# A gated recurrent step with sigmoid gates and one scan, and small work moved between engines, in a four-layer graph kernel

## The reference

```
layer 0:   per edge (i, j): g = exp(coeff*(e_ij - offsets)^2), h = ssp(W1 g + b1), Wf = W2 h + b2
           y_i = sum_j  A_ij^2 * Wf_ij * (Wa r_j);  out = Wd2 ssp(Wd1 y + bd1) + bd2
layer 1:   scores = QK/sqrt(128) + adj; softmax over the 8 largest; weighted sum of V; layer norm
layer 2:   graph attention with leaky scores, masked softmax, normalisation
layer 3:   d = row sum of (adj + I);  d_inv = d > 0 ? d^-0.5 : 0;  agg = d_inv * (adj + I) * d_inv @ x
           dyn = conv1d(x);  LSTM over the 128 positions of dyn, batch 64:
               z = W_ih x_t + b_ih + W_hh h + b_hh;  i, f, g, o = split(z)
               c = sigmoid(f)*c + sigmoid(i)*tanh(g);   h = sigmoid(o)*tanh(c)
           out = sigmoid(agg @ all h)
```

## Time and profile before

| | us |
|---|---|
| median of three runs (1372.89 to 1377.21) | 1374.94 |
| the profiled execution | 1368.68 |
| its span, from the first to the last instruction | 1366.4 |
| PE busy (share of the span) | 1142.1 (84%) |
| DVE busy | 927.6 (68%) |
| ACT busy | 908.8 (67%) |
| POOL busy | 686.5 (50%) |
| mean granted TensorE clock, share of full | 0.957 |

### The profile page before, as it was taken

How to read it: one execution, slowest core, us unless ns; L and a number is a source line. 1 busy time by engine, 2 the same in 40 slices (tenths; PEclk the granted TensorE clock), 3 DMA queues, 4 the chain that set the end, 5 groups by cost and what they waited for, 6 DMA issues and landing times. The chain is left out here.

```text
span 1366.4 us, 28761 instructions
## 1 busy us (share of the span) xinstructions
PE 1142.1 (84%) x5996; PEld 752.7 (55%) x6028; DVE 927.6 (68%) x3952; ACT 908.8 (67%) x2636; POOL 686.5 (50%) x1146
## 2 busy tenths in 40 slices
PE   2588889898988888988925789989789999999984
PEld 1244445555544554555514577777666666666673
DVE  3599998988898988889724888788423333333357
ACT  2488888778788878778812778878544444444467
POOL 5266665656665656656755899998500000000026
PEclk9999999999999999999965999999999999999988
DMA  1788677677777886767700111111000000000003
GB/s 47 162 182 193 167 191 168 174 186 163 172 188 167 187 171 173 191 160 177 172 6 21 34 38 39 32 40 32 16 1 0 0 0 0 0 0 0 0 23 102
DMA packets 128163, 129.04 MB, mean 94 GB/s; under 512 B 60867, under 2 KB 107359, under 8 KB 128097
## 3 DMA queue, kind: packets, MB, share of 16 engines
q1 hardware_dynamic: 126372, 127.19, 38.8%
q10 hardware_dynamic: 1725, 1.13, 0.3%
HBM read 123.05 MB, written 5.21 MB: 94 GB/s over the span
## 5 line engine op out<-in xcount | busy, mean ns | idle before, releaser
L782 PE MATMUL wf<-hid,w2t 128*128 128x384 f32 x512 | 209.3, 534 | 61.6 <-DVE msg L957 61.6
L569 POOL TENSOR_TENSOR sum<-msg 128x384 f32<-128x384 f32 (+1 forms) x128 | 146.5, 1145 | 74.4 <-DVE msg L957 73.9
L782 PEld LDWEIGHTS wf<-hid,w2t 128*128 128x128 f32 x512 | 89.9, 195 | 138.3 <-issue 106.5
L1787 POOL MEMSET r_minus_half<- 128x4 f32 x1 | 0.1, 102 | 324.7 <-POOLq L1653 324.7
L957 DVE SCALAR_TENSOR_TENSOR msg<-wf,b2c,rv 128x768 f32<-128x768 f32 x128 | 130.0, 1015 | 14.6 <-PE wf L782 14.2
L1735 DVE SCALAR_TENSOR_TENSOR r_new<-r_gates 128x64 f32<-128x64 f32 x128 | 28.9, 226 | 149.9 <-ACT r_gates L1715 149.9
L682 ACT ACTIVATE expd<-zb,safe_b,reached 128x768 f32<-128x768 f32 x128 | 124.9, 976 | 1.8 <-PE zb L768 1.8
L930 DVE TENSOR_TENSOR rv<-rg,sq_bc 128x768 f32<-128x768 f32 x128 | 121.4, 948 | 1.7 <-PE rg L811 1.4
L1681 PE MATMUL r_zgo<-xin,w_hh 128*128 (+1 forms) x508 | 110.2, 299 | 14.0 <-DVE xin L1744 1.8
L687 ACT ACTIVATE hid<-expd 128x768 f32<-128x768 f32 x128 | 108.0, 844 | 17.7
L767 PE MATMUL zb<-gauss,w1t 64*128 64x384 f32 x256 | 117.5, 540 | 0.0
(11 more groups left out here) (300 smaller groups left out, 3297.5 us busy)
## 6 DMA issues: line engine op xcount, KB each, us to landing
sq_bc<-edge_sq SPq DMA_DIRECT2D x64, 768.0 KB, 4.4
val_bc<-edge_val SPq DMA_DIRECT2D x128, 192.0 KB, 4.6
idx_bc<-edge_idx SPq DMA_DIRECT2D x64, 384.0 KB, 5.5
adj_w<-in_adj_rows SPq DMA_DIRECT2D x64, 64.0 KB, 5.2
xt_w<-in_x_cols SPq DMA_DIRECT2D x64, 64.0 KB, 4.8
xin<-in_x_rows SPq DMA_DIRECT2D x32, 128.0 KB, 4.7
m_adj_g<-in_adj_rows SPq DMA_DIRECT2D x16, 256.0 KB, 2.7
m_adjt_g<-in_adj_t SPq DMA_DIRECT2D x16, 256.0 KB, 2.7
```

The source lines that it names most:

```text
L569: pool.tensor_tensor(sum1[:, 0:wide, :], m[:, 0:wide, :], m[:, wide:2 * wide, :], ALU.add)\
L782: last = pe.matmul(wf[:, half, 0:HALF], w2t[:, :], hid[:, q, half * HALF:(half + 1) * HALF], start=True, stop=True)
```

## The change

It has five parts.

1. **Recurrence.** PE, ACT and DVE take the gates in the order F, G, I, O. ACT takes sigmoid of F, I, O (tanh of G). DVE multiplies F's gate by the cell as soon as F is there, into every second element of `adds`; ACT writes G's gate into the others, and I's gate into every second element of `factors`, whose others stay zero. One `tensor_tensor_scan` over 128 elements (multiply, then add, each element going on from the one before) gives G, then I*G + F*cell, for each of the 64 batch columns: the product and the cell sum in one instruction. h is a plain product. The second idle matmul has 128 columns. The factors 0.5 and 0.25 on weights, biases and `lw` go.
2. **`prepare_gates`.** The six scalings of biases become one copy, the seven scalings of weights go.
3. **Layer 0.** `over_t` is built by ACT as relu(1 - |number - row|) in two instructions, at the end of `k_in` 0, and DVE writes `over_row` with its sign turned. The sign check leaves ACT: POOL marks entries below zero and adds them up (two instructions per graph, at the head of `k_in` 1). SP waits for that too before it loads an adjacency again.
4. **Checks.** The power -0.5 is taken by ACT as exp(-0.5*ln d); DVE takes one more reduction.
5. **`layers12`.** The same operations are written in another order on all engines, and some are moved by one step.

The diff, cut to its core (of the reordered `layers12` only the first lines are shown):

```diff
-    for q in range(6):
-        step = pool.tensor_scalar(total[:, q, :], left[:, q, :], 0.5 if q in (0, 1, 3) else 1.0, None, ALU.mult)
-    step.then_inc(prep, 1)
+    pool.tensor_copy(total[:, :, :], left[:, :, :]).then_inc(prep, 1)
     pool.wait_ge(prep, 3)
...
-    for q in range(4):
-        pool.tensor_scalar(w_hh[:, q, :], w_hh[:, q, :], 0.5 if q == 2 else 0.25, None, ALU.mult)
-        if q != 2:
-            pool.tensor_scalar(w_ih[:, q, :], w_ih[:, q, :], 0.5, None, ALU.mult)
 
...
+                            after(sp, "below_ready", g, 3, 0)
...
+                        pool.tensor_scalar(below_zero[:, :], adj_w[:, q, :], 0.0, None, ALU.is_lt)\
+                            .then_inc(s["below_ready"], 1)
+                        w(pool, "below_ready", g.at(4) + 1)
+                        pool.tensor_tensor(negatives[:, :], negatives[:, :], below_zero[:, :], ALU.add)\
+                            .then_inc(s["negative_ready"], 1)
...
-                        act.activation(minus[:, :], adj_w[:, q, :], ACT.Relu, scale=-1.0,
-                                       accum_out=least[:, bass.ds(g.at(4), 1)])
...
+                    if not dense and k_in == 0 and g.has(0):
+                        w(act, "row_ready", g.at() + 1)
+                        after(act, "over_t_ready", g, -1, 0)
+                        act.activation(over_gap[:, :], iota_row[:, :], ACT.Abs, bias=over_row[:, bass.ds(g.at(), 1)])\
+                            .then_inc(s["gap_ready"], 1)
+                        w(act, "gap_ready", g.at() + 1)
+                        after(act, "u_ready", g, -2, 0)
+                        act.activation(over_t[:, g.mod(2), :], over_gap[:, :], ACT.Relu, scale=-1.0, bias=1.0)\
+                            .then_inc(s["over_t_ready"], 1)
...
-                dve.tensor_copy(over_row[:, bass.ds(g.at(4), 1)], p_over[:, 2 * RANKS + 1:2 * RANKS + 2])
+                dve.tensor_scalar(over_row[:, bass.ds(g.at(4), 1)], p_over[:, 2 * RANKS + 1:2 * RANKS + 2], -1.0, None,
+                                  ALU.mult).then_inc(s["row_ready"], 1)
...
-                    if not dense and k_in == 1 and g.has(0):
-
-                        after(dve, "u_ready", g, -2, 0)
-                        dve.tensor_scalar(over_t[:, g.mod(2), :], iota_parts[:, :, 0:OPEN_COLS // 3],
-                                          over_row[:, bass.ds(g.at(), 1)], None, ALU.is_equal)\
-                            .then_inc(s["over_t_ready"], 1)
...
-            dve.tensor_scalar(bad[:, 2, :], least[:, :], 0.0, None, ALU.is_gt)
+            dve.tensor_reduce(least[:, :], negatives[:, :], AX.X, ALU.max).then_inc(chk[3], 1)
+            dve.wait_ge(chk[3], 1)
+            dve.tensor_scalar(bad[:, 2, :], least[:, :].broadcast_to((P, B)), 0.0, None, ALU.is_gt)
...
-            pool.wait_ge(powers[0], 1)
-            pool.tensor_tensor(dpow[:, :], dsafe[:, :], k["minus_half"][:, :], ALU.pow).then_inc(powers[2], 1)
-            pool.wait_ge(powers[1], 1)
-            pool.wait_ge(powers[2], 1)
+            pool.tensor_scalar(dsafe[:, :], k["deg"][:, :], 1.0, 1.2e-38, ALU.add, ALU.max).then_inc(safe_ready, 1)
+            pool.tensor_scalar(dpos[:, :], k["deg"][:, :], 1.0, 0.0, ALU.add, ALU.is_gt).then_inc(pos_ready, 1)
+            pool.wait_ge(pos_ready, 1)
+            pool.wait_ge(pow_ready, 1)
             pool.sem_inc(k["held"]["Pool"], 1)
             pool.tensor_tensor(k["dinv"][:, :], dpow[:, :], dpos[:, :], ALU.mult)
+
+        @block.scalar
+        def _(act):
+            act.wait_ge(safe_ready, 1)
+            act.activation(dlog[:, :], dsafe[:, :], ACT.Ln).then_inc(log_ready, 1)
+            act.wait_ge(log_ready, 1)
+            act.activation(dpow[:, :], dlog[:, :], ACT.Exp, scale=-0.5).then_inc(pow_ready, 1)
...
-                    g = step - 5
-                    if 0 <= g < NGR:
-                        w(pool, "rsum2", g)
-                        pool.tensor_tensor(rmask[:, :], rsum2[:, :], mask[:, g * G:(g + 1) * G], ALU.mult).then_inc(s["rmask"], 1)
...
 
-                    for q, ready in ((G_, zg_ready), (I_, zi_ready), (F_, zf_ready), (O_, zo_ready)):
+                    for q, ready in ((F_, zf_ready), (G_, zg_ready), (I_, zi_ready), (O_, zo_ready)):
...
-                        pe.matmul(idle_p[:, 0:2 * P], idle[:, 0:P], idle[:, 0:2 * P], start=True, stop=True)
+                        pe.matmul(idle_p[:, 0:P], idle[:, 0:P], idle[:, 0:P], start=True, stop=True)
...
-                        act.wait_ge(zg_ready, n)
+                        act.wait_ge(zf_ready, n)
                         if not (first and j == 0):
                             act.wait_ge(h_ready, t + j)
-                        act.activation(gates[:, 0, :], z_of(bank, G_)[:, j, :], ACT.Tanh).then_inc(g_ready, 1)
+                        act.activation(forget[:, :], z_of(bank, F_)[:, j, :], ACT.Sigmoid).then_inc(f_ready, 1)
+                        act.wait_ge(zg_ready, n)
+                        act.activation(adds[:, :, 0], z_of(bank, G_)[:, j, :], ACT.Tanh).then_inc(g_ready, 1)
                         act.wait_ge(zi_ready, n)
-                        act.activation(gates[:, 1, :], z_of(bank, I_)[:, j, :], ACT.Tanh).then_inc(i_ready, 1)
-                        act.wait_ge(zf_ready, n)
-                        act.activation(gates[:, 2, :], z_of(bank, F_)[:, j, :], ACT.Tanh).then_inc(f_ready, 1)
+                        act.activation(factors[:, :, 1], z_of(bank, I_)[:, j, :], ACT.Sigmoid).then_inc(i_ready, 1)
                         act.wait_ge(zo_ready, n)
-                        act.activation(gates[:, 3, :], z_of(bank, O_)[:, j, :], ACT.Tanh)
+                        act.activation(gate_o[:, :], z_of(bank, O_)[:, j, :], ACT.Sigmoid)
                         act.wait_ge(cell_ready, n)
...
                 quads(act, body)
 
             @block.vector
             def _(dve):
-                dve.memset(cell[:, :], 0.0)
+                dve.memset(cell[:, :, :], 0.0)
+                dve.memset(factors[:, :, :], 0.0)
                 dve.memset(idle[:, :], 0.0)
                 dve.memset(h0[:, :], 0.0).then_inc(start_ready, 1)
 
                 def body(t, bank, first, final):
                     for j in range(4):
                         n = t + (j + 1)
+                        dve.wait_ge(f_ready, n)
+                        dve.tensor_tensor(adds[:, :, 1], forget[:, :], cell[:, :, 1], ALU.mult).then_inc(keep_ready, 1)
+                        dve.wait_ge(keep_ready, n)
                         dve.wait_ge(g_ready, n)
                         dve.wait_ge(i_ready, n)
-                        dve.scalar_tensor_tensor(new[:, :], gates[:, 1, :], 1.0, gates[:, 0, :], ALU.add, ALU.mult)\
-                            .then_inc(new_ready, 1)
-                        dve.wait_ge(f_ready, n)
-                        dve.scalar_tensor_tensor(keep[:, :], gates[:, 2, :], 1.0, cell[:, :], ALU.add, ALU.mult)\
-                            .then_inc(keep_ready, 1)
-                        dve.wait_ge(keep_ready, n)
-                        dve.scalar_tensor_tensor(cell[:, :], keep[:, :], 0.5, new[:, :], ALU.mult, ALU.add)\
+                        dve.tensor_tensor_scan(cell[:, :, :].rearrange("p b a -> p (b a)"),
+                                               factors[:, :, :].rearrange("p b a -> p (b a)"),
+                                               adds[:, :, :].rearrange("p b a -> p (b a)"), 0.0, ALU.mult, ALU.add)\
                             .then_inc(cell_ready, 1)
                         dve.wait_ge(tanh_ready, n)
-                        dve.scalar_tensor_tensor(hs[:, bass.ds(t + j, 1), :].rearrange("p a b -> p (a b)"),
-                                                 gates[:, 3, :], 1.0, tanh_c[:, :],
-                                                 ALU.add, ALU.mult).then_inc(h_ready, 1)
+                        dve.tensor_tensor(hs[:, bass.ds(t + j, 1), :].rearrange("p a b -> p (a b)"),
+                                          gate_o[:, :], tanh_c[:, :], ALU.mult).then_inc(h_ready, 1)
                 quads(dve, body)
 
...
-                        act.activation(lw[:, g % 2, :, :], lwt_b[g % 2][:, :, :], ACT.Copy, scale=0.5)\
+                        act.activation(lw[:, g % 2, :, :], lwt_b[g % 2][:, :, :], ACT.Copy)\
```

More of the change, by code:

```diff
@@ L1263, in _ @@
                         w(act, "l_p", g)
+                        w(act, "a_self", g)
                         for j in range(G):
@@ new lines, in _ @@
+                    g = step - 4
+                    if 0 <= g < NGR:
+                        pe.matmul(p_l[:, :, :], att_neigh[:, :], x2t[:, :, :], start=True, stop=True).then_inc(s["l_p"], 1)
+                    g = step - 2
+                    if 0 <= g < NGR:
+                        for j in range(G):
+                            last = pe.matmul(p_val[:, j, :], x1t[:, j, :], wvc[:, :], start=True, stop=True)
+                        last.then_inc(s["val_p"], 1)
+                    g = step - 5
```

508 lines of the change are left out of this document (255 added, 253 removed).

## The result

| | before | changed |
|---|---|---|
| median, us | 1376.08 (4 runs) | 1491.68 (4 runs, 1481.73 to 1511.08) |
| profiled execution, its span | 1366.4 | 1483.4 |
| mean granted TensorE clock | 0.957 | 0.844 |

The account below looks back on a forecast made before the run. Limits differed by stage: POOL at the start, in checks and `layers12`, DVE in layer 0, a dependency chain in the recurrence. Terms -5.7 - 15 - 10.0 - 4 + 4.5 = -30.2 took 1374.94 to 1345 us, range 1330 to 1355.

Parts of the forecast that it names:

- part 5: The prediction's section on the recurrence: new chain with the scan, +4.5 us; the shorter filler just fits, otherwise +5.
- E: Rival in the recurrence: scan waits out its predecessor's whole path, lasting 1.02 us; +74, 1419 us; chance 0.04.
- F: Rival in layer 0: ACT's new work is on the path, +23 in place of -15; 1383 us; chance 0.02.
- start: POOL's preparation at the start: fewer scalings of biases and weights release ACT earlier, -5.7 us.
- layer 0: Layer 0's middle: taking over_t off DVE's stream, which sets the pace, gains -15 us, bounds 0 and -17.
- checks: Checks: replacing POOL's 10.59 us power by ACT activations moves the join earlier, -10.0 us.
- `layers12`: Layers 1 and 2: middle keeps its 14.93 us per step, the ramp gains; -4 us, bounds -9 to +6.
- recurrence at full clock: Recurrence chain: tanh of the cell starts at 1.715 instead of 1.68 us, +4.5 us over 128 positions.
- plain rate: Recurrence: scan priced like a plain 128-element instruction, 0.30 us, giving the lower end of -2.6 us.
- B: Rival: layer 0 gives nothing back because PE or ACT takes over the pace, +15; 1360 us; chance 0.13.
- C: Rival in the recurrence: scan takes three slots per element, 0.59 us, +18.6; 1363 us; chance 0.09.
- D: Rival: `layers12` loses its period as PE waits each step, 8, and the ramp gives nothing, 4; 1357 us; chance 0.08.

Follow-up runs that it names:

- a_fill512: The change, order F, G, I, O, with the 512 idle columns multiplied in PE's pause ahead of O and the 128 at the end: 1346.97 us, ratio 0.982.
- b_l12: The kernel before with only the new order of layers 1 and 2: 1368.32 us, ratio 0.997.
- a_idle256: The change with only its second idle matmul back at 256 columns: 1350.79 us, ratio 0.985.
- b_overt: The kernel before with only over_t made by ACT in two activations instead of by DVE: 1357.55 us, ratio 0.987.
- b_sign: The kernel before with only the sign check made by POOL in two instructions per graph instead of by ACT: 1369.10 us, ratio 0.996.
- a_plain_pre: a_plain with one table load, holding sigmoid and tanh, put ahead of the recurrence: 1340.92 us, ratio 0.979.
- a_gfio_pre: The change with gates ordered G, F, I, O, scan kept, 768 idle columns and one table load ahead of the recurrence: 1347.14 us.
- a_plain: The change with gates ordered G, I, F, O, three plain instructions replacing product and scan, and 768 idle columns: 1501.12 us, ratio 1.094.

## Why the prediction was wrong, step by step

**The step that failed** is in part 5: "the idle matmul has half the columns ... So the filler just fits; if it doesn't, 0.04 x 128 = +5." I took the filler as something that takes up room in PE's queue and asked only whether it fits. I didn't ask what it is there for. The earlier trace rows had the answer in view: the clock at 1.00 in the recurrence, where PE was busy for 277 of 291 us, filled up with zeros, and at 0.77 in the ramp, where it wasn't. I read the clock as a property of the stage and carried it over. The two levels give the missing term: a position is 2.50 us at one and 3.86 at the other, and a kernel that falls in the first quarter pays (453.6 - 320.8) = 132.8 us. The forecast had no rival with it; the two that ended slower than before, E and F, were the scan's price and ACT's new work. And I had written the other half down as harmless: "G is now read second ... O starts at 0.97". This moved O by 0.23 us and cost the chain nothing, but it is the second pause, and a_fill512 shows that with it covered the same 640 columns hold the clock. The start, layer 0 and the checks moved the way that was forecast; that the kernel ended slower is this one term, taken as 0 and measured as +132.8.

The steps one by one, apart from the clock:

| term | forecast | measured | from |
|---|---|---|---|
| start | -5.7 | -5.6 | ACT's release 29.55, then 23.97 |
| layer 0 | -15 | -12.7 | means of 12 profiles with the change (655.8, from 650.0 to 661.4) and 6 without (668.5, from 666.0 to 670.5) |
| checks | -10.0 | -10.2 | end of layer 0 to the statistics: 19.95, then 9.75 |
| `layers12` | -4 | -1.4, alone -4.4 | mean of the same 12, 282.4 (279.6 to 285.4), against 283.8 in the profile of before; b_l12 |
| recurrence at full clock | +4.5 | +5.7 | 320.8 against 315.1 |
| sum | -30.2 | -24.2 | medians, a_idle256 against before: -21.4 |
| clock | 0 | +132.8 | the change's recurrence against that of a_idle256 |

**The start** went by its two rows; ACT's first wait behind POOL (compare):

```profile
16.11 0.81 POOL L184 COPY bias_row<-bias_row 1x768 f32<-1x768 f32 x1
...
23.97 0.63 ACT L652 ACTIVATE m_ident<-ident 128x512 f32<-128x512 f32 x1 [5.36 <-POOL safe_b L532]
```

**The checks** too (compare); `dinv` and the flag now end 0.3 us apart:

```profile
681.00 0.48 POOL L1018 TENSOR_SCALAR dsafe<-deg 128x64 f32<-128x64 f32 x1 [3.35 <-SPq L990]
...
681.80 0.26 ACT L1030 ACTIVATE dpow<-dlog 128x64 f32<-128x64 f32 x1
...
682.24 0.32 POOL L1023 TENSOR_TENSOR dinv<-dpow,dpos 128x64 f32<-128x64 f32 x1 [0.21 <-ACT dpow L1030]
...
682.68 0.15 DVE L1014 CAST flag<-mb 1x1 int32<-1x1 f32 x1 [0.28 <-PE mb L1035]
...
690.75 0.87 DVE L1501 BATCH_NORM_STATS2 m_stats_n<-xres 128x6 f32<-128x128 f32 x4 [7.93 <-PEq L139]
```

**Layer 0**: the two edits alone are worth -15.1 and -3.6, together only -12.7. One thing gets dearer when they come together: `pick` on DVE, by line over 60 to 675 us, in b_overt and in the change:

```profile
L932 DVE TENSOR_SCALAR pick<-idx_bc,iota_col 128x768 bf16<-128x768 bf16 x126 | 65.0, 516 | 9.8 <-PE rg L821 9.7
```

```profile
L937 DVE TENSOR_SCALAR pick<-idx_bc,iota_col 128x768 bf16<-128x768 bf16 x125 | 69.3, 554 | 9.8 <-PE rg L826 9.4 <-issue 0.4
```

38 ns x 128 = 4.9 us of DVE's own stream, the full one, while POOL is busy for 448 us of this stretch instead of 394. b_sign has it in part (530 ns, POOL 439 us; the kernel before 521 and 381). But POOL's busy time can't be the whole cause: in the twelve kernels with the same layer 0 it is 430 to 442 us from 60 to 660, and `pick` takes 549 to 635 ns on average. What slows it is open, and the missing 6 us are no larger than the interval of b_overt's own gain. The forecast looked at POOL's idle time and put its new work at nothing. It also read ACT's two activations as at most 0.31 us each; the first took 0.40 and the second 0.31.

**The scan** lasts 425 ns on average, against 0.44 taken:

```profile
L1758 DVE TENSOR_TENSOR_SCAN r_cell<-r_factors,r_adds 128x128 f32<-128x128 f32 x83 | 35.2, 425 | 49.8 <-ACT r_factors L1736 49.8
```

The plain rate, 0.30, is refuted; by the rule in the Trainium skill, "DVE: opcode table, instruction layouts, handler registers and perf-mode slots", section 6 (half throughput), the trace agrees. It starts 0.13 after ACT's last gate where 0.11 was taken, tanh starts 1.73 after PE's first matmul (forecast 1.71), O at 0.97 as forecast. The scan is no gain: a_plain_pre against a_gfio_pre is 1340.92 against 1347.14, with recurrences of 315.4 and 320.1 us. The forecast set its duration against those of two instructions, but the first of these (`new`, I times G) ran beside ACT's last gate, and the scan starts only behind it.

**The rivals.** None came: layer 0 gave its gain (not B, not F), the scan took 0.42 us (not C, not E), `layers12` kept its period (not D). What happened was among none of them; the 0.02 "for what I don't see" had to hold it.

## What to carry to other kernels

Where an engine is kept busy with work whose result nobody reads, find out what that work buys before you cut it, and ask it again when its surroundings change: here a third of the filler could go in one order of gates, and not even a twelfth (64 columns) in another, each by one execution. A clock that depends on what the engine did had only two levels here, so price it as a rival with its full cost (3.86 against 2.50 us per position), however small the edit. If a filler can't be made to hold, take it out: at half clock it is in the way. Look for new pauses on such an engine, also in the first round of a loop, where a table load hides.

## What the runs showed of the hardware

- The half clock keeps itself. In the change PE is busy for 98.7 of the 100 us from 1100 to 1200, at 0.50, and the clock doesn't rise again before the recurrence ends; a_plain and a_plain_pre do the same matmuls, one at half clock to the end and one at full. A half clock from before the recurrence did come back, in the course of six long matmuls that the program issues between its stages, whose result nobody reads either (L163). In the change:

```profile
969.94 4.25 PE L163 MATMUL m_p_s<-m_gamma,m_wqk 128*128 128x512 f32 x6 [3.25 <-issue]
```

```profile
970.00:972.00 2.00, 2.00 (x3) 0.96 (x4) 0.00 (x0) 0.00 (x0) 0.00 (x0) 0.50 0.00 0
972.00:974.00 2.00, 2.00 (x5) 0.60 (x3) 0.00 (x0) 0.00 (x0) 0.00 (x0) 0.80 0.00 0
```

  From 974 us on, where the recurrence begins, it was 1.00.

- A steady loop can lose its clock late: after 17 us without filler, after 25, 58, 68 and 73 us in four forms of F first (one profile each), with positions before that which look alike. A look at the loop's first microseconds says nothing of its rest.
- Two pauses of PE per position took the clock with 640 and 704 idle columns and not with 768; one longer pause didn't, with 512 or 640, and did without any.
- `ACT_TABLE_LOAD` took 1.28 us in each row where it stands; the position around it took 3.46 us (972.63 to 976.09) instead of 2.3. ACT began its next gate 1.32 us after the end of the one ahead of the load (973.22 to 974.54).
